# Non-local attention block on one core: the head's first g chunks in two banks, and left sums by transposes

## The reference, cut to what matters

```
xn = group_norm(x)                             # 32 groups of channels
g  = g_w @ xn + g_b                            # 256 -> 128 channels
f  = xn^T xn                                   # 4096 x 4096 for each image
y  = softmax(f, over keys) @ g^T               # 4096 x 128
wy = W_w @ y + W_b                             # 128 -> 256 channels
out = x + batch_norm(wy) * gamma + beta + xn
```

## Time and profile before

| | |
|---|---|
| time, 3 runs | median 2225.02 us (2223.76 to 2226.59) |
| the profiled execution | 2227.25 us, its span 2225.5 us |
| PE busy | 2082.0 us (94%), 9460 instructions |
| DVE busy | 1527.1 us (69%) |
| ACT busy | 1096.3 us (49%) |
| POOL busy | 813.5 us (37%) |
| mean granted clock of TensorE | 0.982 |

### The profile page before, as it was taken

How to read it: one execution, slowest core, us unless ns; L and a number is a source line. 1 busy time by engine, 2 the same in 40 slices (tenths; PEclk the granted TensorE clock), 3 DMA queues, 4 the chain that set the end, 5 groups by cost and what they waited for, 6 DMA issues and landing times.

```text
span 2225.5 us, 32504 instructions
## 1 busy us (share of the span) xinstructions
PE 2082.0 (94%) x9460; PEld 1487.4 (67%) x9460; DVE 1527.1 (69%) x3095; ACT 1096.3 (49%) x2234; POOL 813.5 (37%) x624
## 2 busy tenths in 40 slices
PE   5899999999999999999999999998999999999988
PEld 4687776755687777665668677675658777666433
DVE  5576666777766766686766666677776677667656
ACT  3344545556444444546544454555544444454645
POOL 3002223459502023447730222355950102345750
PEclk9999999999999999999999999999999999999989
DMA  3112233555512323464531223455541132336969
GB/s 137 76 76 87 99 114 128 166 152 166 185 45 90 112 74 109 142 199 133 174 106 78 86 100 114 128 175 155 172 167 62 72 119 90 119 119 222 333 234 359
DMA packets 108410, 304.53 MB, mean 137 GB/s; under 512 B 11584, under 2 KB 11968, under 8 KB 93888
## 3 DMA queue, kind: packets, MB, share of 16 engines
q1 hardware_dynamic: 108224, 302.30, 39.7%
HBM read 159.65 MB, written 142.61 MB: 136 GB/s over the span
## 4 chain that ended last, share of the span: by engine, by line
PE 67%; issue 11%; POOL 10%; DVE 4%; ACT 4%; DMA 3%; SPq 0%; DVEq 0%; POOLq 0%; ACTq 0%
PE bank L1199 11%; PE bank L1133 9%; PE bank L1135 9%; PE bank L1134 9%; PE bank L1175 8%; PE bank L1203 4%; PE bank L1205 4%; PE bank L1204 4%; POOL fy_d L694 4%; POOL fy_c L694 3%; PE bank L1349 3%; ACT ring L760 2%; PE bank L1270 2%; DMA fy_d<-spill 2%; POOL xl L667 2%
## 5 line engine op out<-in xcount | busy, mean ns | idle before, releaser
L786 ACT CAST phi<-bank 128x512 fp32r<-128x512 f32 x480 | 280.8, 587 | 779.0 <-PE bank L1175 778.4
L930 DVE TENSOR_SCALAR_CACHE_REDUCE ring<-bank 128x512 f32<-128x512 f32 x576 | 395.9, 687 | 245.2 <-PE bank L1135 200.4
L1133 PE MATMUL bank<-xh 128*128 128x512 f32 (+3 forms) x1152 | 521.2, 452 | 7.3 <-POOL xl L667 6.4
L1135 PE MATMUL bank<-xh,xl 128*128 128x512 f32 (+3 forms) x1152 | 439.1, 381 | 0.0
L965 DVE TENSOR_TENSOR plo<-bank,phi 128x512 fp32r<-128x512 f32 x480 | 325.7, 684 | 161.7 <-ACT phi L786 123.7
L1134 PE MATMUL bank<-xl,xh 128*128 128x512 f32 (+3 forms) x1152 | 436.4, 379 | 0.0
L1175 PEld LDWEIGHTS bank<-ident,ring 128*128 128x128 f32 x1920 | 233.6, 142 | 199.4 <-issue 130.0
L1175 PE MATMUL bank<-ident,ring 128*128 128x128 f32 x1920 | 295.5, 277 | 61.4 <-DVE plo L965 31.2
L760 ACT ACTIVATE ring<-ring,nmax 128x512 f32<-128x512 f32 x480 | 344.7, 720 | 0.0
L694 POOL TENSOR_TENSOR fy_c<-fy_c,maxrow 128x512 f32<-128x512 f32 x200 | 261.9, 1312 | 146.9 <-DMA fy_c<-spill 146.5
L694 POOL TENSOR_TENSOR fy_d<-fy_d,maxrow 128x512 f32<-128x512 f32 x188 | 243.0, 1295 | 190.4 <-DMA fy_d<-spill 190.3
(11 more groups left out here) (115 smaller groups left out, 2720.7 us busy)
## 6 DMA issues: line engine op xcount, KB each, us to landing
spill<-ring SPq DMA_DIRECT2D x112, 1024.0 KB, 4.4
fy_c<-spill SPq DMA_DIRECT2D x200, 256.0 KB, 4.6
fy_d<-spill SPq DMA_DIRECT2D x188, 256.0 KB, 4.2
ring<-x_dram SPq DMA_DIRECT2D x40, 512.0 KB, 4.6
lbuf<-spill SPq DMA_DIRECT2D x60, 256.0 KB, 3.8
yd<-yn SPq DMA_DIRECT2D x32, 256.0 KB, 3.4
fx_a<-x_dram SPq DMA_DIRECT2D x16, 512.0 KB, 8.6
out_dram<-fx_a SPq DMA_DIRECT2D x16, 512.0 KB, 5.4
```

What stands on the lines that cost most here:

```text
L786: nc.scalar.copy(phi[:, HI_BUF[n], :], whole(p)).then_inc(hi_made, 1)
L930: last = nc.vector.tensor_scalar(ring[:, SLOT[u], t, :], src, 1.0, None, ALU.mult, ALU.max, accum_out=rowm[:, t, c:c + 1])
L1133: nc.tensor.matmul(dst, xh[:, k, rows], xh[:, k, cols], start=(k == 0), stop=False)
L1135: last = nc.tensor.matmul(dst, xl[:, k, rows], xh[:, k, cols], start=False, stop=(k == K - 1))
```

## The change

In the head, the first four chunks of g (`FIRST_G`, 0 to 3) are made before step 0 and no longer in steps 2, 3, 6 and 7. Half 0 goes into the shared bank and half 1 into `lacc`, so PE waits for the take of the half before the last one. On ACT, the copies of chunks 0 and 1 come after the first exps, in step -2; those of chunks 2 and 3 stay where they were, at steps 4 and 8. Everywhere, the left sums are made by four transposes into the whole shared bank and a DVE sum of 512 numbers in each partition to 4 (into a new tile lside), which is then added to the right sums. The tile of ones and its memset go.

```diff
+FIRST_G = range(LAST_HEAD_G[0])
...
-            for c in NEXT_G:
-                make_gh(0, c, first=True)
             for s in range(FIRST_EXP, 0):
                 for x3 in EXPS_AT[s]:
                     exp_right(0, *x3)
+                if s + LAG == 0:
+                    for c in NEXT_G:
+                        make_gh(0, c, first=True)
...
+            def add_g(n, c, h, first=False):
                 dve.wait_ge(g_made, n * (2 * NB) + 2 * c + h + 1)
+                made = lacc if first and h == 1 and c in FIRST_G else sps
...
                     dve.wait_ge(left_summed, b * (NB - 1) + j)
-                    nc.vector.tensor_tensor(lsum[:, :], sps[:, 0:2 * T].rearrange("p (t o) -> p t o", o=2)[:, :, 0],
-                                            lsum[:, :], ALU.add).then_inc(summed, 1)
+                    nc.vector.tensor_reduce(lside[:, :], sps.rearrange("p (t m) -> p t m", t=T), AX.X, ALU.add
+                                            ).then_inc(side_summed, 1)
+                    dve.wait_ge(side_summed, b * (NB - 1) + j)
+                    nc.vector.tensor_tensor(lsum[:, :], lside[:, :], lsum[:, :], ALU.add).then_inc(summed, 1)
...
-                if p - 1 in G_AT:
+                if p - 1 in G_AT and not (first and G_AT[p - 1][0] in FIRST_G):
                     add_g(b, *G_AT[p - 1])
...
-            for c in NEXT_G:
+            for c in FIRST_G:
                 for h in range(2):
-                    add_g(0, c, h)
+                    add_g(0, c, h, first=True)
...
-                elif c + h > 0:
-                    pe.wait_ge(g_added, 2 * c + h)
+                elif c > 0:
+                    pe.wait_ge(g_added, 2 * c + h - (1 if c in FIRST_G else 0))
+                made = lacc if first and h == 1 and c in FIRST_G else sps
...
-                    last = nc.tensor.matmul(sps[:, 2 * t:2 * t + 2], lsb[:, t * P:(t + 1) * P], ones[:, :],
-                                            start=True, stop=True)
+                    last = nc.tensor.transpose(sps[:, t * P:(t + 1) * P], lsb[:, t * P:(t + 1) * P], ident[:, :])
...
-                if p in G_AT:
+                if p in G_AT and not (first and G_AT[p][0] in FIRST_G):
                     make_g(b, *G_AT[p], first)
...
-            for c in NEXT_G:
+            for c in FIRST_G:
                 for h in range(2):
                     make_g(0, c, h, first=True)
```

More of the change, by code:

```diff
@@ L421, in nonlocal_block @@
         gavg = sb("gavg", [P, P])
-        ones = sb("ones", [P, 2])
         wgs = sb("wgs", [P, K, 2 * CI], F32R)
@@ L439, in nonlocal_block @@
         lsum = sb("lsum", [P, T])
+        lside = sb("lside", [P, T])
         linv = sb("linv", [P, T])
@@ L494, in nonlocal_block @@
         left_summed = sem("left_summed")
+        side_summed = sem("side_summed")
         summed = sem("summed")
@@ L698, in _ @@
             nc.gpsimd.memset(neghalf[:, :], -0.5)
-            nc.gpsimd.memset(ones[:, :], 1.0)
             nc.gpsimd.memset(ident[:, :], 0.0)
@@ L906, in group @@
                                             1.0, None, ALU.add).then_inc(gnp_made, 1)
-            def add_g(n, c, h):
+            def add_g(n, c, h, first=False):
                 dve.wait_ge(g_made, n * (2 * NB) + 2 * c + h + 1)
-                nc.vector.tensor_reduce(gf[:, c, 2 * h:2 * h + 2, :], sps.rearrange("p (t o c) -> p t c o", t=T // 2, o=2),
+                made = lacc if first and h == 1 and c in FIRST_G else sps
+                nc.vector.tensor_reduce(gf[:, c, 2 * h:2 * h + 2, :], made.rearrange("p (t o c) -> p t c o", t=T // 2, o=2),
                                         AX.X, ALU.add).then_inc(g_added, 1)
@@ L1147, in make_g @@
                     shared_free(b, "g", c, h)
-                elif c + h > 0:
-                    pe.wait_ge(g_added, 2 * c + h)
+                elif c > 0:
+                    pe.wait_ge(g_added, 2 * c + h - (1 if c in FIRST_G else 0))
+                made = lacc if first and h == 1 and c in FIRST_G else sps
                 for r in range(2 * h, 2 * h + 2):
                     rows = slice(c * W + r * P, c * W + (r + 1) * P)
-                    both = sps[:, r % 2 * 2 * CI:(r % 2 + 1) * 2 * CI]
-                    high = sps[:, r % 2 * 2 * CI:r % 2 * 2 * CI + CI]
+                    both = made[:, r % 2 * 2 * CI:(r % 2 + 1) * 2 * CI]
+                    high = made[:, r % 2 * 2 * CI:r % 2 * 2 * CI + CI]
                     nc.tensor.matmul(both, xh[:, 0, rows], wgs[:, 0, :], start=True, stop=False)
```

## The result

| | before | after |
|---|---|---|
| time, 4 runs each | median 2225.81 us (2223.76 to 2232.47) | median 2203.72 us (2198.53 to 2206.03) |
| ratio | | 0.9892 (0.9865 to 0.9920) |
| the profiled execution, its span | 2227.25, 2225.5 us | 2198.53, 2196.8 us |
| mean granted clock, profiled execution | 0.982 | 0.991 |

0.9892 of 2225.02 us is 2201 us: 24 us gained where 16.9 were forecast, just past the lower end of the range.

What follows compares the result with a forecast made beforehand. PE was taken as the main bound (67% of the chain, POOL 10%). Head -10.9 and left sums -6.0 gave -16.9 us, from a median of 2225.02 to 2208 us, range 2202 to 2218.

Steps and rivals of the forecast that it cites:

- The head: Before and in the first steps: earlier first turn 3.57, clock 3.15, halves gone 3.68, waits gone 0.49; 10.9 us saved.
- The term for the clock: In the head, 87 to 95 us: PE stays at 2.4 GHz, 3.15 us come back (bounds nothing and 3.15).
- PE at the left sums: Row group ends: transposes take PE 0.37 us less on 20 sums, 7.4 us; nothing in POOL's stretches.
- DVE at the left sums: Reduction adds about 0.72 us, mostly hidden; half of three row group 4 sums' delay counted, 1.1 us (bounds 0, 2.2).
- The net path of the sums: All left sums: -7.4 on PE, +1.1 on DVE, +0.35 at the last sum, about -6.0 us.
- The bound of +9.8: Left sums' slow bound: every DVE delay reaches PE, 28 x 0.35 us.
- the first rival: DVE bounds the row groups' ends: all delays reach PE, 2224 (chance 0.05); about half, 2214 (0.11).
- The clock at the left sums: Transposes among products at the left sums do not bring the clock down; no clock gain or loss in the sum.
- falls that vanish: More gain than forecast, with clock falls vanishing and sums in cold stretches gaining about double: 2198 to 2204, chance 0.05.
- DVE as the bound: At the row groups' ends DVE sets the pace: 2224 if all 28 delays reach PE (0.05), 2214 if half (0.11).
- That the head gives less: In the head the clock falls anyway, or DVE and ACT pace the steps: 7.7 us or less, 2211; chance 0.15.
- The third, slower by more falls: Clock falls after each left sum on PE's stretches, 2.3 us each, 48 us on 21 sums: 2256; chance 0.04.

Runs made afterwards that it cites:

- head only: Kernel before with only the head's part (four chunks of g in two banks, exps ahead of the copies), left sums as before: 2216.2 us, ratio 0.9949.
- one transpose: Kernel before with one transpose of ones in place of each left sum's four 2-column matmuls, so DVE adds 1: 2199.2 us, ratio 0.9889.
- side sums in the bank: Changed kernel, but DVE writes its sums of 512 to 4 into the shared bank instead of an SBUF tile: 2198.6 us, 0.9889 of the kernel before.
- the sums alone: Kernel before with only the left sums changed to four transposes and a DVE sum, head as before: 2213.7 us, ratio 0.9945.
- eight transposes: Kernel with only the left sums changed, each sum's four transposes made twice: 2222.4 us, 0.9975 of the kernel before.

## Why the prediction was right and wrong

**The head (10.9 us): right.** With the later start of this execution taken off, each start named in it came within 0.3 us, and step 12 is 10.9 us ahead. The take of the half before the last paces the pairs at 1.97 us (77.75 to 79.72), as worked out. It passed to the end in full: in head only the lead changes by about 0.1 us or less from row group to row group wherever neither trace falls. The term for the clock was taken at 3.15 us; by cold time head only has 12.7 us less, 5 us at 0.40, so it was a little small, and its path is -7.1 for 7.7.

**PE at the left sums (0.37 us each): slightly small.** Four transposes took 0.36 where the next work is a product (248.65 to 249.01 in the changed kernel), so 0.45. The sums in POOL's stretches gave nothing, as forecast: the gain of row group 4 is lost again in row group 5, where DVE sets the pace.

**DVE at the left sums (1.1 us, "I take half of 3 x 0.72"): mis-sized.** Row group 5 loses 1.54 us in each of three images, 4.6 us. 0.45 of the 1.54 are PE's own gain, which doesn't pass where DVE is the bound (one transpose, with nothing added on DVE, loses 0.85 there, all of the 0.8 that it had gained). About 0.75 are the reduction and its wait (side sums in the bank: 1.2 in all), and 0.35 the longer add. The whole delay reached PE, not half, and with the longer add it is 3 x 1.1 = 3.3 us where the term was 1.1 and its upper bound 2.2. The net path of the sums was -4.3, not -6.0. The bound of +9.8, on which the first rival's times rest, credits PE's 0.37 us to all 28 sums where the sum has it for 20; with 20 it is 28 x 0.72 - 7.4 = 12.8.

**The clock at the left sums (0 us): the step that failed.** The prediction put the falls behind the head down to chance: "Where the falls of the clock lie differs from run to run, worth some 2 us either way". Where they lie does differ. How long they last is not chance alone: it depends on what PE does behind the wait for the exps (11 of 13 over 6 us with 2-column matmuls, 0 of 14 with transposes). It read the stretch at 1.00 only as proof that transposes do no harm, and did not ask what the 2-column matmuls did in the stretch at 0.93 right above it, though each of the two falls that reach into it has eight of them in it (at 786.75 and 858.25 us). 24 us less cold, about 9.6 us: with it -4.3 becomes the -12 to -14 measured for the sums alone, and the sum of the two parts, 11.3 + 12.2 = 23.5, is the 24 us of the result. The prediction gave 0.05 to a gain of this size by "falls that vanish"; the time landed there, but the falls got shorter and did not vanish, and no term of the sum held it. Why such narrow matmuls keep the clock down stays open; what is shown is that they do.

**The rivals.** DVE as the bound holds in one row group of eight, not in all. That the head gives less did not come. The third, slower by more falls, was backwards: cold time fell to about half. Its price of 2.3 us a fall was too low as well: the 10.0 us cold that it divides are only the parts inside the stretch of two falls that last 10.2 and 6.8 us. The Trainium skill, "TensorE: Matmul & The Clock Gate", section "Part 4: PE-mode transpose", says that transpose-mode work does not bring the full clock; here the clock rises right behind eight transposes and not behind eight 2-column matmuls of the same length, so the measurement decides against the rule, at least against its use for this trade.

## What to carry to other kernels

Ask of each matmul behind a wait of PE not only what it takes but what it does for the clock: a few narrow float32 matmuls just behind an idle stretch cost 0.8 us by themselves and, where the clock had fallen, several times that in the work at 1.2 GHz that follows (from the sum to the spreading of the inverse 8.36 us behind them, 5.33 us behind eight transposes, at the place shown above). Count the cold time of the whole trace and look at which instructions stand in it; if the long falls all hold one kind of instruction, their length is not chance. An engine that is idle for 30% of the span, as DVE is here, can still be the bound for 9 us behind one row group: there its delays pass in full, and the other engines' gains don't.

## What the runs showed of the hardware

- An add of 128x4 numbers on DVE took 0.16 us with one input in PSUM and 0.16 to 1.25 us (mean 0.59) with both inputs in SBUF, in the changed kernel. All 22 adds that were longer than 0.16 us began while POOL worked on a tile of 128x512 (about 1.3 us or longer) and ended 0.01 to 0.03 us after it did; the other six began while POOL was not in such a tile. The Trainium skill, "SBUF — State Buffer", section "SBUF: two separate sides", says that a VectorE instruction with two SBUF inputs and a GpSimd instruction that reads SBUF lock each other out for the whole of an instruction, which fits; putting one input in PSUM brought all 28 back to 0.16 us.
- Cold time costs 0.40 us for each microsecond at 1.2 GHz here, not 0.50 (perhaps because PE waits for others in part of it, which was not measured); the two stretches of the earlier trace rows had given 0.45.
- Executions of one kernel differ by up to 1% (2216 to 2240 us for the kernel before), and nearly 80% of the variance of its 54 executions goes with the mean clock.
